# A mixture-of-experts layer beside spiking attention: finding each expert's rows by inverting the permutation on chip and gathering them, in place of scattering them to a sorted table

## The chip, the cores and the metric

The kernel runs on one core of a Trainium2 chip. The metric is the time of one execution on the device, in microseconds (us). Engines are named as in the profile: PE (TensorE), DVE (VectorE), ACT (ScalarE), POOL (GpSimd) and SP (SyncE, which only issues DMAs here). Each engine works through its own program in order and waits on semaphores for the others.

## The reference, cut to what matters

The input is `x` of shape (2, 2048, 256): 4096 tokens. Both halves read the normalized rows `xn` and are added to `x`.

```python
xn = (x - mean(x)) / sqrt(var(x) + 1e-5)
# attention: spikes of layer-normed projections, 16 heads, a distance bias, no softmax
Q, K, V = (lif(layer_norm(xn @ W.T + b, g, beta), 1.0) for each of q, k, v)
out = lif(((16 - hamming(Q, K) + log_pe_bias) * scale) @ V, 0.5)
attn = lif(layer_norm(out @ Wo.T + bo, go, betao), 1.0)
# experts: 8 of them, each token goes to its 2 best
probs = softmax(xn @ router_w.T)
scores, expert_idx = top_k(probs, 2); scores /= sum(scores)
h = xn @ up_proj[e]                      # 256 -> 512
hidden = silu(h[..., :256]) * h[..., 256:]
ffn = sum over the 2 experts of score * (hidden @ down_proj[e])
result = x + attn + ffn
```

Each expert computes only the rows that chose it. There are 8192 (token, choice) pairs. They are sorted by expert and each expert's share is padded to a multiple of 128, so that they fill `SLOT_TILES` = 71 tiles of 128 slots (9088 slots, 896 of them pads).

## The kernel before, in words

A token tile is 128 tokens; there are `NT` = 32, and even and odd tiles belong to the two batches. The program has four stretches.

1. Load and route. `x` is loaded into `xn` and normalized there (`stats`, L768), turned by PE into `xT`, multiplied with the router weights and turned back (L1105 to L1130). DVE picks the two best experts of each token (`pick`), PE counts with a triangular matrix (`ranks`), and DVE works out for each token and choice the slot in the sorted order: `pos`, written at L882, which signals `placed`.
2. Projections. `project_and_sum` on PE, one token tile a step: 3 groups (q, k, v) of a bias matmul (L1160) and six weight matmuls (`three`, L1085 to L1087, a high and a low half of each operand), the turn of the q spikes of the tile four steps back (L1148) and its share of the k-v sum (L1169). ACT keeps the high half of the next tile (`keep_xh`, L432), squares the results (L479) and keeps the turned q (L467). DVE subtracts for the low half (`keep_xl`, L776), finishes the deviations (L924 to L930) and compares for spikes (L941); `project` on DVE handles in step t the spikes of the pair before. `project` on PE for tile t waits for the low half of tile t, and for the spikes of tile t-4, since two sets of three PSUM banks are shared in turn. Between steps ACT and DVE split the expert weights into halves (L436, L918). DVE calls `rest_of_routing` (L886 to L906) between the first pair's spikes and step 4: it finds the owner of each slot tile, and where the pads go.
3. Experts, 71 slot tiles. While the projections run, POOL scatters: for each token tile and each choice an indirect DMA writes 128 rows of `xn` to their slots of the DRAM table `slot_x` (L658, 64 of them), and 7 more write pad rows (L665). Each row carries two more columns: where its result goes, and its first expert. SP waits for all of the scatter (`scattered`) and then loads the table tile by tile into four places `ex` (L340, `load_tile`), each as soon as PE has turned the tile that lay there. PE turns a tile (`turn_ex`, L1212) two tiles ahead, ACT and DVE keep its halves (L524, L910), PE multiplies up, ACT and DVE apply silu and the product (L519, L973), PE turns and multiplies down, ACT stores `ey` (L535), and POOL sends the rows to their places in `slot_y` with an indirect DMA (L673, `send`). DVE computes the destinations of the rows from the two columns (`row_places`, L987). ACT's `keep_y` waits until the send four tiles back has landed. `xres`, the input again for the last addition, is loaded between the tiles (L350).
4. Attention over 16 blocks of 128 positions of both batches, then output projection and the three additions. SP loads `y_tok` from `slot_y` when every send has landed (L366). POOL takes part with L684, L692 and L699.

The order on each engine is written out by hand, with hardware loops (`steps`, `Fori`) where steps repeat. The DVE steps around the change stand so:

```python
deviations(0, 0, 0); spikes(0, 0, 0); keep_xl(4, 4); spikes(0, 0, 1)
dve.wait_ge(s["bias_set"], 1)
rest_of_routing()
for lo, hi, n in PIECE_ROUNDS:      # (4, 16, 8), (16, 28, 14)
    steps(dve, lo, hi, ... project ...)
```

Of the kernel before, what the change touches and what calls it, by code (L numbers as in the profile page):

```python
# [16 lines left out]
P = 128  # L17
# [11 lines left out]
PADS = SLOTS - B * N * TOPK  # L29
PC = PADS // P  # L30
ROW = D + 2
Y_ROWS = TOPK * B * N + 2 * PADS
# [8 lines left out]
BELOW_ALL = -3.0e38  # L41
OFFSETS = [0, 1, -1, 2, -2, 4, -4, 8, -8]
WARM = 16
POOL_PIECES = 8
PEEL, ROUND = 4, 4
KV_OPEN = 2
PIECE_SETS = [(0, 8), (8, 18), (18, 22), (22, PIECES)]
WEIGHT_PIECE, LGT_PIECE, BIAS_PIECE, ROUTE_PIECE, PAD_PIECE = 8, 12, 16, 18, 22
# [3 lines left out]
PAD_TILE = 3  # L52
# [15 lines left out]
def spiking_moe(nc, x, w_all, router, bias, gain, beta, scale, experts, ident, ident_b, toep, far_map, far_pick,  # L68
                head_mask, before, route_const, pad_mark, out):
    with ExitStack() as ctx:  # L70
# [4 lines left out]
        slot_x = nc.dram_tensor("slot_x", (SLOTS, ROW), F32, kind="Internal").ap()  # L75
# [4 lines left out]
        slot_x_tiles = slot_x.rearrange("(j p) d -> p j d", p=P)  # L80
        y_pairs = slot_y[0:TOPK * B * N, :].rearrange("(b a p k) d -> p a b (k d)", b=B, a=NB, k=TOPK)
# [36 lines left out]
        pos = keep("pos", [P, TOPK, NT], I32)  # L118
        owner_f = keep("owner_f", [P, SLOT_TILES])
        owner = keep("owner", [P, SLOT_TILES], I32)  # L120
        pad_i = keep("pad_i", [P, PC], I32)
# [4 lines left out]
        dest = keep("dest", [P, 4], I32)  # L126
# [4 lines left out]
        xn = place_in(r_x)("xn", [P, NT, ROW])  # L131
        xres = place_in(r_x)("xres", [P, NT, D])

# [29 lines left out]
        pos_f = put("pos_f", [P, TOPK, NT])  # L163
# [3 lines left out]
        pad_w = put("pad_w", [P, PC, E])  # L167
        pad_f = put("pad_f", [P, PC])
        rc = put("rc", [P, route_const.shape[1]])
        assert ends[piece_at(ROUTE_PIECE)] <= piece_at(PAD_PIECE)  # L170
        put = place_in(piece_at(PAD_PIECE))
        pad_rows = put("pad_rows", [P, PC, ROW])
        w_rt = put("w_rt", [P, KC, E])
        assert ends[piece_at(PAD_PIECE)] <= piece_at(PIECES)
# [4 lines left out]


# [11 lines left out]
        ex = place_in(r_e)("ex", [P, 4, ROW])  # L192
# [27 lines left out]
        def part(bank, h):  # L220
# [8 lines left out]
        q_ps = banks[6][:, 0:P].bitcast(BF16)  # L229
        kv_ps = banks[7]  # L230
# [13 lines left out]
            chosen_set ranked gap_set gate_exp gates_set placed pads_placed pads_marked pads_done scattered  # L244
            q_turned xh_set xl_set qT_set proj_done ssq_done std_done heron spk_done kv_done
            piece_h piece_l pool_piece far_built far_set half_summed kv_less kv_set kv_fixed
            ex_turned exh_set exl_set sends_begun up_done gact_done hid_done hid_turned hidh_set hidl_set down_done ey_done dest_done
# [6 lines left out]
        ex_in = [sem(f"ex_in{i}") for i in range(4)]  # L254
        y_out = [sem(f"y_out{i}") for i in range(4)]
# [50 lines left out]
        def _(sp):  # L306
# [16 lines left out]
            load_pieces(0)  # L323
            sp.wait_ge(s["routed"], 1)
            sp.wait_ge(s["xn_done"], NT)
# [4 lines left out]
            sp.wait_ge(s["pads_placed"], 1)  # L330
            load_pieces(2)
            sp.wait_ge(s["pads_done"], 16 * PC)
# [3 lines left out]
            def load_tile(j, slot):  # L336
                if not early(j, 4):
                    sp.wait_ge(s["ex_turned"], j - 3)
                    sp.wait_ge(s["dest_done"], j - 3)
                sp.dma_start(ex[:, slot, :], entry(slot_x_tiles, j)).then_inc(ex_in[slot], 16)  # L340

            sp.wait_ge(s["scattered"], 16 * TOPK * NT)
            for j in range(8):
                load_tile(j, j % 4)
# [4 lines left out]
            with sp.Fori(0, QUADS - 2) as i:  # L349
                sp.dma_start(xres[:, bass.ds(i * B, B), :], x_pairs[:, bass.ds(i, 1), :, :].rearrange("p a b d -> p (a b) d")).then_inc(s["xres_in"], 16)  # L350
                for u in range(4):
                    load_tile(i * 4 + (8 + u), u)
            for j in range(4 * QUADS, SLOT_TILES):
                load_tile(j, j % 4)
            for a in range(QUADS - 2, NB):
                sp.dma_start(xres[:, a * B:(a + 1) * B, :], x_pairs[:, a, :, :]).then_inc(s["xres_in"], 16)
# [1070 lines left out]
```

## Time and profile before

| what | us |
|---|---|
| median of 3 runs | 443.77 (443.08 to 443.96) |
| the profiled execution | 444.79 |
| its span, first to last instruction | 442.9 |
| PE busy | 378.5 (85%) |
| DVE, ACT, POOL busy | 273.0, 232.5, 214.5 |

The profiled execution took 444.79 us, of which the profile's span covers 442.9; 1.9 us lie around it. Times in the views are us from the start of the span. PE's matmuls are pipelined, so a busy PE is not PE at its peak. The "granted clock" is the share of full speed that the chip gave PE; 0.5 is 1.2 GHz and 1.0 is 2.4 GHz.

### The profile page before, as it was taken

What the parts mean: (1) busy time and instruction counts of PE and PEld (TensorE: products, weight loads), DVE (VectorE), ACT (ScalarE), POOL (GpSimd) and SP (SyncE); (2) the same over time, 40 slices, a digit from 0 to 9 for tenths busy, and PEclk for the clock granted to TensorE, in tenths of its full rate; (3) what the DMA queues carried; (4) which work ended last, traced back from release to release, by engine and by line L of the source; (5) the groups of instructions that cost most, each with busy time, mean ns of one, the idle gap of its engine ahead of it and who ended that gap; (6) DMA issues with size and microseconds to landing.
All of it is one profiled execution on the core that took longest, in us unless ns stands there. A gap on an engine that the chain in (4) does not pass through costs nothing.

```text
span 442.9 us, 9338 instructions
## 1 busy us (share of the span) xinstructions
PE 378.5 (85%) x2521; PEld 306.0 (69%) x2522; DVE 273.0 (62%) x774; ACT 232.5 (52%) x752; POOL 214.5 (48%) x213
## 2 busy tenths in 40 slices
PE   5388958999999508999999999999999998999840
PEld 1223657999999506778888888888888875666630
DVE  5796899777778505454445545444554434479994
ACT  1436835888888504544455455445445434466650
POOL 5215336777777750333333333333333332489993
PEclk9796979999999956999999999999999999999995
DMA  8880063424222231533334334333334413982222
GB/s 256 257 285 1 10 228 101 174 91 150 95 101 103 95 109 48 169 118 122 119 125 124 119 119 130 120 122 126 121 119 121 115 61 109 382 319 96 95 73 95
DMA packets 40108, 58.93 MB, mean 133 GB/s; under 512 B 5974, under 2 KB 27606, under 8 KB 40088
## 3 DMA queue, kind: packets, MB, share of 16 engines
q1 hardware_dynamic: 31392, 38.53, 27.6%
q0 software_dynamic: 6848, 18.70, 11.6%
q10 hardware_dynamic: 1848, 1.47, 1.1%
q8 instruction: 9, 0.15, 0.1%
q14 instruction: 11, 0.09, 0.1%
HBM read 35.79 MB, written 22.89 MB: 132 GB/s over the span
## 4 chain that ended last, share of the span: by engine, by line
PE 41%; POOL 26%; issue 13%; DMA 6%; DVE 5%; ACT 4%; SPq 3%; DVEq 0%; POOLq 0%; ACTq 0%
POOL slot_x L658 14%; PE bank L1085 12%; PE bank L1087 11%; PE bank L1086 11%; POOL xres L699 4%; POOL xres L692 3%; SPq L309 3%; PE bank L1212 3%; PE bank L1228 3%; DMA ew_f<-experts 2%; DMA vec_d<-two_col 2%; DVE exT_l L910 2%; POOL slot_x L665 2%; ACT gact L519 2%; DMA ex<-slot_x 1%
## 5 line engine op out<-in xcount | busy, mean ns | idle before, releaser
L673 POOL DMA_INDIRECT slot_y<-ey,dest x71 | 68.5, 965 | 139.7 <-ACT ey L535 111.4
L973 DVE TENSOR_TENSOR hid<-gact,bank 128x256 f32<-128x256 f32 x71 | 29.9, 421 | 77.6 <-ACT gact L519 77.6
L658 POOL DMA_INDIRECT slot_x<-xn,pos x64 | 64.7, 1011 | 25.6 <-issue 19.2
L1085 PE MATMUL bank<-ew,exT_h 128*128 x142 | 63.6, 448 | 5.3 <-DVE exT_l L910 5.2
L519 ACT ACTIVATE gact<-bank 128x256 f32<-128x256 f32 x71 | 27.4, 386 | 65.7 <-PE bank L1087 65.7
L1087 PE MATMUL bank<-ew,exT_l 128*128 x142 | 56.9, 401 | 0.0
L1086 PE MATMUL bank<-ew,exT_h 128*128 x142 | 56.8, 400 | 0.0
L1085 PE MATMUL bank<-w_h,xT_h 128*128 128x256 f32 x192 | 54.3, 283 | 0.0
L1087 PE MATMUL bank<-w_h,xT_l 128*128 128x256 f32 x192 | 54.1, 282 | 0.0
L1086 PE MATMUL bank<-w_l,xT_h 128*128 128x256 f32 x192 | 54.1, 282 | 0.0
L1085 PE MATMUL bank<-ew,hidT_h 128*128 x142 | 45.7, 322 | 1.0 <-DVE hidT_l L977 1.0
L479 ACT ACTIVATE junk<-bank 128x256 bf16<-128x256 f32 x96 | 35.8, 379 | 19.3 <-PE bank L1087 18.9
L529 ACT ACTIVATE hidT_h<-bank 128x256 fp32r<-128x256 f32 x71 | 27.3, 385 | 33.5 <-PE bank L1228 33.5
L977 DVE TENSOR_TENSOR hidT_l<-bank,hidT_h 128x256 fp32r<-128x256 f32 x71 | 30.1, 425 | 21.3 <-ACT hidT_h L529 21.3
L1212 PE MATMUL bank<-id_f,ex 128*128 128x128 f32 x142 | 27.7, 279 | 15.9 <-DMA ex<-slot_x 15.9
L910 DVE TENSOR_TENSOR exT_l<-bank,exT_h 128x256 fp32r<-128x256 f32 x71 | 29.7, 418 | 17.4 <-ACT exT_h L524 17.4
L1087 PE MATMUL bank<-ew,hidT_l 128*128 x142 | 40.0, 281 | 0.0
L1086 PE MATMUL bank<-ew,hidT_h 128*128 x142 | 39.9, 281 | 0.0
L1212 PEld LDWEIGHTS bank<-id_f,ex 128*128 128x128 f32 x142 | 20.2, 144 | 26.2 <-DMA ex<-slot_x 16.5
L1085 PEld LDWEIGHTS bank<-w_h,xT_h 128*128 128x128 f32 x192 | 37.3, 194 | 0.0
L1086 PEld LDWEIGHTS bank<-w_l,xT_h 128*128 128x128 f32 x192 | 37.1, 193 | 0.0
L1087 PEld LDWEIGHTS bank<-w_h,xT_l 128*128 128x128 f32 x192 | 37.0, 193 | 0.0
(183 smaller groups left out, 967.4 us busy)
## 6 DMA issues: line engine op xcount, KB each, us to landing
ex<-slot_x SPq DMA_DIRECT2D x71, 129.0 KB, 2.0
y_tok<-slot_y SPq DMA_DIRECT2D x8, 1024.0 KB, 14.1
xres<-x SPq DMA_DIRECT2D x16, 256.0 KB, 2.7
out<-xres SPq DMA_DIRECT2D x16, 256.0 KB, 2.1
xn<-x SPq DMA_DIRECT2D x6, 512.0 KB, 11.7
ew_f<-experts SPq DMA_DIRECT2D x1, 2560.0 KB, 10.1
ew_f<-experts SPq DMA_DIRECT2D x1, 2048.0 KB, 10.3
slot_y<-ey,dest POOLq DMA_INDIRECT x71, 2.4
```

Source lines behind the costliest of these rows:

```text
L479: nc.scalar.activation(junk[:, i, :], proj_ps[r][i], ACT.Square, accum_out=ssq[:, r, i:i + 1]).then_inc(s["ssq_done"], 1)
L519: nc.scalar.activation(gact[:, m % 2, :], h_ps[m % 2][:, 0:F], ACT.Silu).then_inc(s["gact_done"], 1)
L529: nc.scalar.activation(flat2(hidT_h[:, m % 2, :, :]), hT_ps[m % 2], ACT.Copy).then_inc(s["hidh_set"], 1)
L658: pool.indirect_dma_start(slot_x, bass.IndirectOffsetOnAxis(ap=pos[:, k, t:t + 1], axis=0), xn[:, t, :], None).then_inc(s["scattered"], 16)
L673: pool.indirect_dma_start(slot_y, bass.IndirectOffsetOnAxis(ap=dest[:, m % 4:m % 4 + 1], axis=0), ey[:, m % 4, :], None).then_inc(y_out[m ...
L910: v.tensor_tensor(flat2(exT_l[:, m % 2, :, :]), ex_ps[m % 2], flat2(exT_h[:, m % 2, :, :]).bitcast(F32), ALU.subtract).then_inc(s["exl_set ...
L973: v.tensor_tensor(hid[:, m % 2, :], gact[:, m % 2, :], h_ps[m % 2][:, F:2 * F], ALU.mult).then_inc(s["hid_done"], 1)
L977: v.tensor_tensor(flat2(hidT_l[:, m % 2, :, :]), hT_ps[m % 2], flat2(hidT_h[:, m % 2, :, :]).bitcast(F32), ALU.subtract).then_inc(s["hidl_ ...
L1085: mm(dst, a_h, b_h, start=first, stop=False)
L1086: mm(dst, a_h, b_l, start=False, stop=False)
L1087: return mm(dst, a_l, b_h, start=False, stop=last)
L1212: last = turn(ex_ps[m % 2][:, c * P:(c + 1) * P], ex[:, u, c * P:(c + 1) * P], id_f[:, :])
```

## The change

The table `slot_x`, the scatter, the pad rows and the two extra columns go. Instead the normalized rows are written plainly to a DRAM copy `xn_d`, and each slot tile is gathered from it by the slots' token numbers. For that the map from tokens to slots has to be inverted. For each of 64 (choice, token tile) pairs DVE builds two one-hot masks, `in_row` (128 tokens by 128 lanes: the slot's place in its tile) and `in_tile` (128 tokens by 71 tiles, once times the pair's number and once times the token's lane), and PE multiplies the one with the other and sums all 64 products in `inv_ps` (128 lanes by 142). This is done in 4 sets of 16, spread over the DVE steps 4 to 7, which are written out now; PE does its 64 matmuls after step 7 and waits there until DVE has read the result. From it DVE computes `token` (what to gather) and `dest` (where the result goes) for all slots at once. POOL gathers 32 tiles into a ring that lies where `xn` lay, then one more after each send. SP copies a gathered tile from the ring to `ex`. `xres` lies over the ring, and is loaded after the last tile.

```diff
+Y_FIRST = 2 * P
+SETS = 4
+PER_SET = TOPK * NT // SETS
+A_PLACES = 3
+RING = NT
-PEEL, ROUND = 4, 4
+PEEL, TURN_STEP, ROUND = 4, 8, 4
...
         @block.sync
             load_pieces(0)
+            for lo, hi in X_CHUNKS:
+                sp.wait_ge(s["xn_done"], hi)
+                sp.dma_start(xn_rows[:, lo:hi, :], xn[:, lo:hi, :]).then_inc(s["xn_out"], 16)
...
-            sp.wait_ge(s["pads_placed"], 1)
+            sp.wait_ge(s["slots_set"], 2)
+            sp.wait_ge(s["owners_set"], 1)
+            sp.wait_ge(s["turned_back"], SETS)
             load_pieces(2)
...
-                if not early(j, 4):
-                    sp.wait_ge(s["ex_turned"], j - 3)
-                    sp.wait_ge(s["dest_done"], j - 3)
-                sp.dma_start(ex[:, slot, :], entry(slot_x_tiles, j)).then_inc(ex_in[slot], 16)
-            sp.wait_ge(s["scattered"], 16 * TOPK * NT)
+                sp.wait_ge(gathered[j % 4], 16 * (j // 4 + 1))
+                if j >= 4:
+                    sp.wait_ge(s["ex_turned"], j - 3)
+                sp.dma_start(ex[:, j % 4, :], xn[:, j % RING, :]).then_inc(ex_in[j % 4], 16)
...
+            for j in range(8, SLOT_TILES):
+                load_tile(j)
+            blocks = [*range((SLOT_TILES - 2 * RING) // B + 1, NB), *range((SLOT_TILES - 2 * RING) // B + 1)]
+            for a in blocks:
+                last = max(k for k in range(SLOT_TILES) if k % RING in (B * a, B * a + 1))
+                sp.wait_ge(s["ex_turned"], last + 1)
                 sp.dma_start(xres[:, a * B:(a + 1) * B, :], x_pairs[:, a, :, :]).then_inc(s["xres_in"], 16)
...
         @block.scalar
+            def scale_in_tile(c):
+                act.wait_ge(s["in_tile_seen"], c + 1)
+                flat = in_tile[:, c, :, 1, :]
+                nc.scalar.activation(flat, flat, ACT.Copy, scale=p_col).then_inc(s["in_tile_set"], 1)
...
+                    for t in range(lo, TURN_STEP):
+                        project(t, t, n + (t - lo) // 2 if t % 2 else None)
+                        scale_in_tile(t - lo)
...
         @block.gpsimd
-            pool.wait_ge(s["placed"], 1)
-            for t in range(NT):
-                for k in range(TOPK):
-                    pool.indirect_dma_start(slot_x, bass.IndirectOffsetOnAxis(ap=pos[:, k, t:t + 1], axis=0),
-                                            xn[:, t, :], None).then_inc(s["scattered"], 16)
...
+            def gather(j):
+                if j >= 4:
+                    pool.wait_ge(gathered[j % 4], 16 * (j // 4))
+                pool.indirect_dma_start(xn[:, j % RING, :], None, xn_d,
+                                        bass.IndirectOffsetOnAxis(ap=token[:, j:j + 1], axis=0)).then_inc(gathered[j % 4], 16)
...
+            pool.wait_ge(s["slots_set"], 2)
+            for j in range(RING):
+                gather(j)
+            for j in range(SLOT_TILES):
+                send(j)
+                if RING + j < SLOT_TILES:
+                    gather(RING + j)
...
         @block.vector
-            v.tensor_copy(pos[:, :, :], pos_f[:, :, :]).then_inc(s["placed"], 1)
-            def rest_of_routing():
...
+            step(v.tensor_copy(pos_i[:, :], pos_f[:, :]))
+            settled()
+            step(v.tensor_scalar(lo_i[:, :], pos_i[:, :], P - 1, None, ALU.bitwise_and))
+            settled()
+            step(v.tensor_copy(lo_f[:, :], lo_i[:, :]))
+            settled()
+            v.tensor_tensor(hi_f[:, :], pos_f[:, :], lo_f[:, :], ALU.subtract).then_inc(s["split"], 1)
+            def mark_tiles(c):
...
+                shape = [P, PER_SET, SLOT_TILES]
+                step(v.tensor_tensor(in_tile[:, c, :, 1, :], hi_f[:, k].unsqueeze(2).broadcast_to(shape),
+                                     tile_start.unsqueeze(1).broadcast_to(shape), ALU.is_equal))
                 settled()
+                v.tensor_tensor(in_tile[:, c, :, 0, :], in_tile[:, c, :, 1, :], choice_no[:, k].unsqueeze(2).broadcast_to(shape),
+                                ALU.mult).then_inc(s["in_tile_seen"], 1)
+            def mark_rows(c):
+                if c >= A_PLACES:
+                    dve.wait_ge(s["turned_back"], c - A_PLACES + 1)
+                k = slice(c * PER_SET, (c + 1) * PER_SET)
+                shape = [P, PER_SET, P]
+                v.tensor_tensor(in_row[:, c % A_PLACES, :, :], lo_f[:, k].unsqueeze(2).broadcast_to(shape),
+                                row_no.unsqueeze(1).broadcast_to(shape), ALU.is_equal).then_inc(s["in_row_set"], 1)
+            def owners():
...
+            def slots():
+                dve.wait_ge(s["turned_back"], SETS)
...
+                v.tensor_scalar(token[:, :], place, -float(P), 0.0, ALU.add, ALU.max).then_inc(s["slots_set"], 1)
+                v.scalar_tensor_tensor(dest[:, :], place, 2.0, pads, ALU.mult, ALU.add).then_inc(s["slots_set"], 1)
...
-            rest_of_routing()
...
+                    for t in range(lo, TURN_STEP):
+                        mark_tiles(t - lo)
+                        if t - lo < A_PLACES:
+                            mark_rows(t - lo)
+                        project(t, t, None, n + (t - lo) // 2 if t % 2 else None)
+                    owners()
+                    mark_rows(A_PLACES)
+                    slots()
...
-                row_places(j, m, i)
...
         @block.tensor
+            def turn_back(c):
+                if c == 0:
+                    pe.wait_ge(s["qT_set"], TURN_STEP - PEEL)
+                pe.wait_ge(s["in_row_set"], c + 1)
+                pe.wait_ge(s["in_tile_set"], c + 1)
+                for i in range(PER_SET):
+                    last = mm(inv_ps, in_row[:, c % A_PLACES, i, :], in_tile[:, c, i, :, :].rearrange("p a j -> p (a j)"),
+                              start=(c == 0 and i == 0), stop=(c == SETS - 1 and i == PER_SET - 1))
+                last.then_inc(s["turned_back"], 1)
...
-            steps(pe, PEEL, LAST_STEPS, project_and_sum)
+            for t in range(PEEL, TURN_STEP):
+                project_and_sum(t, t, None)
+            for c in range(SETS):
+                turn_back(c)
+            pe.wait_ge(s["slots_read"], 1)
+            steps(pe, TURN_STEP, LAST_STEPS, project_and_sum)
```

`owners` is three of the instructions of `rest_of_routing` (L890, L898, L901). `slots` has three dependent steps of 71 elements ahead of the two that are shown, and the last of the three signals `slots_read`. The masks are bf16, `hi_f`, `lo_f`, `tile_start`, `choice_no` and `row_no` are fp32.

## Rows read from the trace of the kernel before

**Rows 1.** The page, busy time of PE, its share and its instructions.
```profile
PE 378.5 (85%) x2521; PEld 306.0 (69%) x2522; DVE 273.0 (62%) x774; ACT 232.5 (52%) x752; POOL 214.5 (48%) x213
```

**Rows 2.** Chain of work that ended last: start, length, what.
```profile
22.74 10.31 DMA ew_f<-experts
...
68.65 1.06 POOL slot_x L658
...
161.44 2.51 DMA slot_x<-xn,pos
163.97 2.10 DMA ex<-slot_x
166.12 0.70 PE bank L1212 x2
```

**Rows 3.** PE timeline: start, length, line, tiles, count, idle before and its releaser.
```profile
75.27 0.38 PE L1160 MATMUL bank<-bias_r,ones_r 128*128 128x256 f32 x1 [1.34 <-DVE xT_l L776]
...
83.38 0.36 PE L1160 MATMUL bank<-bias_r,ones_r 128*128 128x256 f32 x1
...
149.07 0.28 PE L1169 MATMUL bank<-v_spk,qk_spk 128*128 128x128 bf16 x2
149.19 0.28 PE L1148 MATMUL bank<-id_b,qk_spk 128*128 128x128 bf16 x2
...
150.96 0.27 PE L1169 MATMUL bank<-v_spk,qk_spk 128*128 128x128 bf16 x2
...
175.43 0.48 PE L1085 MATMUL bank<-ew,exT_h 128*128 x1
...
186.00 0.48 PE L1085 MATMUL bank<-ew,exT_h 128*128 x1
...
190.10 0.48 PE L1085 MATMUL bank<-ew,exT_h 128*128 x1
```

**Rows 4.** Windows: stretch, busy time of the engines, granted clock, DMA share, GB/s.
```profile
57.50:61.30 3.80, 0.00 (x0) 0.01 (x1) 3.61 (x7) 2.46 (x8) 1.75 (x2) 0.97 1.03 384
61.30:68.00 6.70, 5.85 (x27) 5.39 (x28) 6.39 (x19) 1.22 (x5) 1.00 (x1) 0.51 0.16 62
...
151.20:166.10 14.90, 0.03 (x1) 0.00 (x0) 0.00 (x0) 0.34 (x1) 8.64 (x9) 0.57 0.32 108
...
167.90:173.60 5.70, 5.66 (x14) 4.34 (x15) 4.06 (x12) 1.82 (x3) 0.00 (x0) 0.50 0.05 9
...
200.00:280.00 80.00, 78.07 (x480) 67.11 (x478) 39.23 (x120) 39.56 (x120) 28.80 (x30) 1.00 0.39 122
```

**Rows 5.** DVE timeline from the routing to step 5 of the projections.
```profile
68.17 0.20 DVE L882 CAST pos<-pos_f 128x64 int32<-128x64 f32 x1
...
71.67 0.16 DVE L886 TENSOR_TENSOR per_e<-per_e 128x8 f32<-128x8 f32 x1
...
71.95 0.67 DVE L890 TENSOR_TENSOR owner_w<-rc,per_e 128x497 f32<-128x497 f32 x1
...
74.71 0.42 DVE L776 TENSOR_TENSOR xT_l<-xT,xT_h 128x256 fp32r<-128x256 f32 x1 [0.26 <-issue]
...
78.59 0.69 DVE L918 TENSOR_TENSOR ew<-ew_f,ew  x1
```

**Rows 6.** Groups by line: tiles, shapes, count, busy, mean ns, idle before.
```profile
L673 POOL DMA_INDIRECT slot_y<-ey,dest x71 | 68.5, 965 | 139.7 <-ACT ey L535 111.4 <-issue 28.3
L658 POOL DMA_INDIRECT slot_x<-xn,pos x64 | 64.7, 1011 | 25.6 <-issue 19.2 <-DVE pos L882 6.4
...
L436 ACT ACTIVATE ew<-ew_f 128x512 fp32r<-128x512 f32 (+1 forms) x24 | 14.7, 620 | 5.0 <-DMA ew_f<-experts 5.0
```

**Rows 7.** DVE timeline where the experts begin.
```profile
167.25 0.42 DVE L910 TENSOR_TENSOR exT_l<-bank,exT_h 128x256 fp32r<-128x256 f32 x1 [17.11 <-ACT exT_h L524]
...
169.47 0.42 DVE L910 TENSOR_TENSOR exT_l<-bank,exT_h 128x256 fp32r<-128x256 f32 x1
```

**Rows 8.** SP's queue, timeline: first issue, time to the last, tiles, count.
```profile
372.19 13.88 SPq L366 DMA_DIRECT2D y_tok<-slot_y  x8
```

More of the change, by code:

```diff
@@ L68, in spiking_moe @@
 def spiking_moe(nc, x, w_all, router, bias, gain, beta, scale, experts, ident, ident_b, toep, far_map, far_pick,
-                head_mask, before, route_const, pad_mark, out):
+                head_mask, before, route_const, out):
     with ExitStack() as ctx:
@@ L117, in spiking_moe @@
         gwork = keep("gwork", [P, 3, NT])
[L118 to L119 removed]
         owner = keep("owner", [P, SLOT_TILES], I32)
[L121 removed]
+        token = keep("token", [P, SLOT_TILES], I32)
+        dest = keep("dest", [P, SLOT_TILES], I32)
         eps_c = keep("eps_c", [P, 1])
@@ L162, in spiking_moe @@
         best = put("best", [P, 4, NT])
-        pos_f = put("pos_f", [P, TOPK, NT])
+        pos_f = put("pos_f", [P, TOPK * NT])
+        lo_f, hi_f = (put(n, [P, TOPK * NT]) for n in ("lo_f", "hi_f"))
+        pos_i = put("pos_i", [P, TOPK * NT], I32)
+        lo_i, hi_i = (put(n, [P, TOPK * NT], I32) for n in ("lo_i", "hi_i"))
+        slot_w = put("slot_w", [P, 4, SLOT_TILES])
         per_e = put("per_e", [P, 8, E])
@@ L178, in spiking_moe @@
         spk = put("spk", [P, NB, B, D])
+        at = sum(CONST_WIDTHS[:4])
+        choice_no = rc[:, at:at + TOPK * NT]
+        row_no = rc[:, at + TOPK * NT:at + TOPK * NT + P]
+        p_col = rc[:, at + TOPK * NT + P:at + TOPK * NT + P + 1]
         r_v = ends[r_w]
@@ L254, in spiking_moe @@
         ex_in = [sem(f"ex_in{i}") for i in range(4)]
+        gathered = [sem(f"gathered{i}") for i in range(4)]
         y_out = [sem(f"y_out{i}") for i in range(4)]
@@ L348, in _ @@
             sp.dma_start(far_s[:, :], far_map).then_inc(s["toep_in"], 16)
[L349 to L355, printed above, removed]
+            for j in range(8, SLOT_TILES):
+                load_tile(j)
+            blocks = [*range((SLOT_TILES - 2 * RING) // B + 1, NB), *range((SLOT_TILES - 2 * RING) // B + 1)]
+            for a in blocks:
+                last = max(k for k in range(SLOT_TILES) if k % RING in (B * a, B * a + 1))
+                sp.wait_ge(s["ex_turned"], last + 1)
                 sp.dma_start(xres[:, a * B:(a + 1) * B, :], x_pairs[:, a, :, :]).then_inc(s["xres_in"], 16)
@@ L620, in _ @@
             g.memset(ones_b[:, :], 1.0).then_inc(s["ones_set"], 1)
-            step(g.memset(pad_rows[:, :, :], 0.0))
             step(g.memset(ones_r[:, :].bitcast(F32), 1.0))
@@ L810, in _ @@
             consts = []
-            for width in (E, E * NT, SLOT_TILES, PC, NT):
+            for width in CONST_WIDTHS[:4]:
                 consts.append(rc[:, at:at + width])
                 at += width
-            rev, keep_run, tile_start, pad_no, y_place = consts
-            step(v.tensor_copy(xn[:, :, D], y_place))
+            rev, keep_run, tile_start, pad_row = consts
             all_te = [P, NT, E]
@@ L839, in _ @@
             step(v.scalar_tensor_tensor(lg2[:, :, :], first[:, :, :], BELOW_ALL, lg, ALU.mult, ALU.add))
-            step(v.tensor_scalar(xn[:, :, D + 1], best[:, 1, :], -1.0, float(E), ALU.mult, ALU.add))
             settled()
@@ L978, in keep_hidl @@
                                 ALU.subtract).then_inc(s["hidl_set"], 1)
-            def row_places(j, m, i):
-                u = m % 4
-                if early(j, 4):
-                    dve.wait_ge(ex_in[u], 16)
-                else:
-                    dve.wait_ge(y_out[u], 16 * i)
-                v.scalar_tensor_tensor(dest[:, u:u + 1], ex[:, u, D + 1:D + 2], cut(owner_f, j, 1), ex[:, u, D:D + 1],
-                                       ALU.not_equal, ALU.add).then_inc(s["dest_done"], 1)
             def expert(j, m, i):
```

112 lines of the change are left out of this document (53 added, 59 removed).

## The prediction

> **What bounds the kernel now.** I read the page first: PE is busy for 85% of the span [rows 1], so a PE idle stretch is what a change can win, and added PE waits are what it can lose. The chain of waits names the idle stretch: from 68.65 it runs through POOL's scatter, 64 + 7 indirect DMAs back to back, to the last one at 161.44; that lands after 2.51, the first tile load takes 2.10, and only then, at 166.12, does PE turn the first expert tile [rows 2]. The PE timeline gives the other side: the last projection work ends at 151.1 [rows 3], so PE stands still for 15.0 us; the window 151.2 to 166.1 has no PE work in it [rows 4]. The next window shows the after-effect: when PE restarts, the granted clock is 0.50 (the 1.2 GHz level) for 5.7 us [rows 4]. From 200 to 280 PE is busy for 78.07 of 80 us at full clock, 480 matmuls, 16 a tile: 30 tiles at 2.67 us each [rows 4]. The experts are bound by PE. Projections are too: from step 8 (83.38) to the end of step 31 (149.07) are 24 steps of 2.74 us [rows 3]. There the DVE timeline matters: two DVE steps (4 and 5) start at 74.71 and end at about 79.2, so 4.5 for two, 2.25 each [rows 5]. DVE has 0.5 us to spare per step of PE. That small reserve is what the new masks draw on.
>
> **What is won where the experts begin.** With the scatter gone, PE passes from the last projection to the first turn at 151.1 instead of 166.12. I follow the same order of instructions at full clock, in times of the old trace. The first low half starts on DVE about 0.9 after that turn begins (1.13 in the trace with the turn at half clock), at 152.0. The second follows 2.2 later, since the last spikes lie between them (167.25 to 169.47, at DVE's own speed [rows 7]), and PE can start its second tile at 154.8. The two tiles' up matmuls took 5.7 at half clock [rows 4], so one takes 1.4 at full; the turn of the last q spikes, an exchange with ACT, took the 1.8 from 173.6 to the third tile at 175.43 [rows 3, 4]. The third tile then starts at 154.8 + 1.4 + 1.8 = 158.0 instead of 175.43: **17.4 won**, 15.0 of waiting and 2.4 of clock. Bounds: 15.0 if PE comes out of the handover at half clock again, 18.5 if its small waits shrink too.
>
> A second gain: the step from tile 6 at 186.00 to tile 7 at 190.10 took 4.10 instead of 2.67 [rows 3], because the tile load stood in SP's queue behind two tables and a part of `xres`. That part moves to the end, and the load no longer waits for `row_places`. **1.4 won**, bounds 0 and 1.4. The removed `row_places` itself is worth nothing: DVE is busy for 39 of 80 us there [rows 4].
>
> **What the masks cost.** They stand in DVE's program between steps that feed PE. The price per element: a compare of 497 elements took 0.67 and an instruction of 8 took 0.16 [rows 5], so 0.16 fixed and 1.04 ns an element. `mark_tiles` is two instructions of 16 x 71 = 1136 elements, 1.35 each, the second waiting for the first: 2.7. `mark_rows` is one of 2048, 2.3, or 2.2 to the next start. Four sets: 4 x (2.7 + 2.2) = 19.5. No mask is in the old trace; below, two results a cycle would give 10; above, 25, if POOL or a broadcast operand slowed them. I take 19.5, by the nearest row, a compare with broadcast operands.
>
> DVE's program now, from the same start: `rest_of_routing` began at 71.67 [rows 5]. Splitting the slot number adds three small dependent instructions like L882's 0.20 [rows 5] and two small copies go: 72.1. Then 19.5 of masks, 9.0 for four steps, and 1.6 for `owners` (two instructions like L890's 0.67 and a small one [rows 5]): 102.2. The last set's 16 matmuls follow on PE: two bf16 matmuls of 128 columns start 0.12 apart [rows 3], so 142 columns take 0.067, the set 1.1. Then DVE's chain up to `slots_read`, four small instructions or waits of 0.2: 0.8. PE begins step 8 at 104.1 instead of 83.38: **20.7 lost**. PE steps 5 to 7 each wait for a low half behind the masks, as step 5 does already for 1.34 [rows 3]. The first three sets (3.3, or 6.6 at half clock) lie under DVE's step 7 and `owners`; with all of it at half clock PE ends later than DVE and the loss is 22.5. Bounds 19 and 22.5 before any clock loss behind it. Nothing is given back later, because steps 8 to 31 run at PE's pace.
>
> The waits have this queue behind them: behind PE's wait for `slots_read` stand all later projections; behind `mark_rows(3)`, waiting for the first set, stand `slots` and DVE's step 8. ACT's four scalings of 1136 elements, 1.4 each if 512 take 0.62 [rows 6], fall where ACT waits for PE; uncovered they would cost 5.5.
>
> The clock: after 3.8 us without PE work (57.5 to 61.3) it was granted 0.51 for 6.7 us, about 3.3 us of work lost [rows 4]. In the new steps 5 to 7 PE stands for 4 to 5 us between projections, so it will fall there, where DVE sets the pace. Behind step 8 it costs 0 if it has recovered during the sets, 3.3 if not. I take **1.0**.
>
> **Parts that I cost at nothing.** The gathers begin at 104.5; 32 at 1.01 + 0.30 [rows 6] end at 146.5, 25 us before the experts. Without that cover each would cost its 1.3. In the expert stretch POOL does a send and a gather a tile for 39 tiles: 0.97 + 0.30 + 1.31 = 2.58 against PE's 2.67 [rows 4, 6]. A gather is not in the trace: below, it is a send's 0.97, above the 2.51 from issue to landing [rows 2]; I take the scatter's, the same instruction the other way round. The plain copy of `xn` (4 MB) is issued behind the load of expert pieces at 22.74, which takes 10.31 [rows 2]; if it stays behind in the same queue it costs nothing and is out by about 50, if it mixed in, up to 4 us. `xres`, again 4 MB, is issued once tile 66 is turned, some 26 us ahead of the reading of `y_tok` at 372.19 [rows 8]; at the 384 GB/s of one window [rows 4] it takes 11. Uncovered: 11. The Trainium skill, in "DMA: Bandwidth & Descriptors", section Queues, rings and completion order, says that each DMA engine takes turns between the queues of the issuers. By it the last sends would share the engines with `xres` and not wait behind all of it, which leaves the sum as it is; no run so far shows it.
>
> **Sum**, for the profiled execution: 444.8 + 20.7 + 1.0 - 17.4 - 1.4 = 447.7. The old median lies 1.0 below its profiled execution, so I forecast **446.7** for the median, 2.9 above the old. By 0.2% (0.9 us), what a measurement of this kernel can tell from no change, that is slower.
>
> **Rivals.** (B) The masks cost less, and the kernel gets faster. Place: DVE in steps 4 to 7. Everything else being as above, it decides from a mask sum below 16.6 instead of 19.5. For it: the masks are written in bf16. Against it: their inputs are fp32, and the compare of 497 elements ran at one a cycle. At two a cycle the masks take 10.2, and the median is 446.7 - 9.3 = 437.4. The Trainium skill, in "VectorE: DVE Perf Modes", section The perf-mode tier table, gives an operation on two tensors twice the rate for bf16 and the single rate for fp32. By the first the time would be the 437.4, by the second my sum; L890 with fp32 on both sides agrees with the second, and bf16 results from fp32 inputs no quiet row shows. (C) PE comes back at half clock at step 8, or in the handover, and pays another 3: 449.5. For it: both earlier restarts did so [rows 4]. Against it: the sets themselves are PE work just ahead. (D) POOL cannot keep the pace: from 1.40 a gather the pair is longer than 2.67. At 1.7 it falls behind by 0.3 a tile, 11.7 in 39 tiles; `keep_y` tolerates a send some three tiles late, 7 us: about 5 more, 451.7. Against it: the scatter's even 1.31. (E) The copy of `xn` delays the expert pieces, on which the early chain hangs [rows 2], by up to 4: 450.7. (F) The change doesn't free the start of the experts, because a gathered tile comes late: the 17.4 stay away and it is 464. The 25 us of cover speak against it.
>
> **How the numbers follow.** The forecast (A) has 0.63, with its own range 443.5 to 449.5; B 0.12, C 0.12, D 0.07, E 0.04, F 0.02. Of A, 0.13 lies at faster (masks or routing shorter by a fifth) and 0.08 within 0.2%; B is faster, and half a share of C to E is eaten by a shorter mask sum, 0.02. Faster 0.27, same 0.09, slower 0.64. The range goes from 440.0, half of B left out, to 452.0, which takes in C, E and most of D.
>
> **What would show it.** Right: PE's step 8 at 104 to 106; the compares at 1.35 and 2.3; PE waiting for DVE three times by 4 to 5 us between 77 and 102; no idle stretch at the experts' start, and full clock there; gathers at 1.3, over by 147; 2.67 a tile as before; the last stretch unchanged. Wrong: masks at 0.7 and 1.2; PE idle ahead of the expert tiles; a tile pace above 2.7 in the first 39 tiles; `ew_f` landing later than 33.

## The result and the profile after

The changed kernel takes **449.37 us** (median of 4, 448.21 to 450.83), the kernel before 443.42 beside it (4 runs, 441.89 to 443.96): a ratio of 1.0153, 95% interval 1.0134 to 1.0173. It is slower by 5.95 us, where I forecast 2.9: right in sign and inside the range, too small by half.

From the page of the changed kernel, the same line as in [rows 1]. TensorE is busy 11 us longer, in 64 more matmuls and in work at the lower clock:
```profile
PE 389.5 (87%) x2585; PEld 318.6 (71%) x2586; DVE 283.8 (64%) x717; ACT 237.0 (53%) x756; POOL 210.7 (47%) x211
```
DVE's timeline, the first set of masks, the next set's first mask, and the last mask with what follows. It answers to [rows 5]; columns are start, length, engine, line, operation, tiles, shapes, and in brackets the idle time before and its releaser:
```profile
72.27 1.34 DVE L916 TENSOR_TENSOR in_tile<-hi_f,rc 128x1136 bf16<-128x1136 f32 x1
73.64 1.35 DVE L919 TENSOR_TENSOR in_tile<-in_tile,rc 128x1136 bf16<-128x1136 bf16 x1
74.90 2.29 DVE L928 TENSOR_TENSOR in_row<-lo_f,rc 128x2048 bf16<-128x2048 f32 x1
...
79.31 1.34 DVE L916 TENSOR_TENSOR in_tile<-hi_f,rc 128x1136 bf16<-128x1136 f32 x1
...
99.55 2.28 DVE L928 TENSOR_TENSOR in_row<-lo_f,rc 128x2048 bf16<-128x2048 f32 x1
104.00 0.23 DVE L945 TENSOR_SCALAR slot_w<-bank 128x71 f32<-128x71 f32 x1 [2.17 <-PE bank L1246]
```
PE's timeline over the same stretch and to tile 7 of the experts, for [rows 3]: the starts of steps 5, 6 and 7, the sets of matmuls that invert the permutation, step 8 and step 9, the last group of step 31, the third expert tile, and the tiles 6 and 7 (counted from 0, as in the prediction):
```profile
77.58 0.38 PE L1207 MATMUL bank<-bias_r,ones_r 128*128 128x256 f32 x1 [2.89 <-DVE xT_l L796]
...
85.09 0.55 PE L1207 MATMUL bank<-bias_r,ones_r 128*128 128x256 f32 x1 [3.01 <-DVE v_spk L990]
...
91.56 0.49 PE L1207 MATMUL bank<-bias_r,ones_r 128*128 128x256 f32 x1 [2.07 <-DVE xT_l L796]
...
95.78 3.21 PE L1246 MATMUL bank<-in_tile,in_row 128*128 128x142 bf16 x48
101.89 2.07 PE L1246 MATMUL bank<-in_tile,in_row 128*128 128x142 bf16 x16 [2.90 <-DVE in_row L928]
105.27 0.39 PE L1195 MATMUL bank<-id_b,qk_spk 128*128 128x128 bf16 x2 [1.30 <-DVE slot_w L950]
...
105.48 0.58 PE L1207 MATMUL bank<-bias_r,ones_r 128*128 128x256 f32 x1
...
109.72 0.36 PE L1207 MATMUL bank<-bias_r,ones_r 128*128 128x256 f32 x1
...
173.21 0.28 PE L1207 MATMUL bank<-bias_r,ones_r 128*128 128x256 f32 x1
...
183.01 0.48 PE L1132 MATMUL bank<-ew,exT_h 128*128 x1
...
193.52 0.48 PE L1132 MATMUL bank<-ew,exT_h 128*128 x1
...
196.05 0.49 PE L1132 MATMUL bank<-ew,exT_h 128*128 x1
```
Windows of the changed kernel, for [rows 4] (stretch, busy time of PE, PEld, DVE, ACT, POOL, then the granted clock, DMA share and GB/s):
```profile
95.00:102.00 7.00, 4.10 (x59) 3.87 (x58) 6.77 (x10) 2.28 (x6) 0.00 (x0) 0.99 0.00 0
102.00:105.00 3.00, 1.97 (x16) 1.68 (x15) 0.93 (x5) 0.00 (x0) 0.00 (x0) 0.50 0.00 0
105.00:112.00 7.00, 6.73 (x46) 6.61 (x47) 3.59 (x14) 3.46 (x13) 4.02 (x4) 0.73 0.76 261
112.00:173.00 61.00, 61.00 (x546) 59.79 (x546) 47.53 (x143) 50.05 (x198) 27.57 (x28) 1.00 0.25 74
173.00:185.00 12.00, 8.74 (x62) 7.05 (x61) 8.27 (x23) 6.68 (x22) 0.00 (x0) 1.00 0.18 56
200.00:280.00 80.00, 78.32 (x483) 67.48 (x482) 35.34 (x90) 39.56 (x120) 58.53 (x61) 1.00 0.45 146
```
POOL at the start of the gathers and in the expert stretch, for [rows 6]:
```profile
105.79 1.17 POOL L682 DMA_INDIRECT xn<-xn_d,token  x1 [43.65 <-DVE dest L955]
107.26 0.95 POOL L682 DMA_INDIRECT xn<-xn_d,token  x1 [0.30 <-issue]
...
187.31 1.00 POOL L688 DMA_INDIRECT slot_y<-ey,dest  x1 [38.67 <-ACT ey L562]
188.62 0.98 POOL L682 DMA_INDIRECT xn<-xn_d,token  x1 [0.30 <-issue]
189.90 1.00 POOL L688 DMA_INDIRECT slot_y<-ey,dest  x1 [0.30 <-issue]
```
The difference, stretch by stretch on PE, after against before:

| stretch | before | after | difference |
|---|---|---|---|
| start to step 8 | 83.38 | 105.48 | +22.1 |
| step 8 to the last group of step 31 | 64.89 | 67.73 | +2.8 |
| last group to the third expert tile | 27.16 | 9.80 | -17.4 |
| third tile to tile 6 | 10.57 | 10.51 | -0.1 |
| tile 6 to tile 7 | 4.10 | 2.53 | -1.6 |
| tile 7 to the last matmul of the experts | 177.01 | 176.17 | -0.8 |
| from there to POOL's last addition into `xres` | 69.73 | 70.23 | +0.5 |

(In the trace of before the last group of step 31 starts at 148.27, the last matmul of the experts at 367.11 and that addition ends at 436.84; after, 372.22 and 442.45.) The sum is +5.6, close to the medians' 5.95. The two profiled spans differ by 3.4 only, since from that last addition to the end the trace of before takes 6.1 and this one 3.9. The traces of all the variants below take 3.8 to 3.9 there; whether 6.1 is usual for the kernel before, its one trace doesn't tell. Its profiled execution (444.79) lies 1.4 above its median, that of the changed kernel (448.21) 1.2 below.

### The profile page after: what moved, and what is told of

It is laid out like the page before. It is cut to its first block, busy times and chain, and to the rows that moved or that the text cites. A ratio compares the mean times of both kernels' runs of the same rounds, so it can differ in the third digit from the quotient of the medians.

```text
span 446.3 us, 8933 instructions
## 1 busy us (share of the span) xinstructions
PE 389.5 (87%) x2585; PEld 318.6 (71%) x2586; DVE 283.8 (64%) x717; ACT 237.0 (53%) x756; POOL 210.7 (47%) x211
## 4 chain that ended last, share of the span: by engine, by line
PE 55%; DVE 15%; issue 9%; POOL 9%; DMA 4%; ACT 3%; SPq 3%; POOLq 0%; DVEq 0%; ACTq 0%
PE bank L1132 15%; PE bank L1134 14%; PE bank L1133 14%; POOL xres L719 4%; POOL xres L712 3%; PE bank L1291 3%; SPq L323 3%; DMA ew_f<-experts 2%; PE bank L1275 2%; PE bank L1207 2%; DVE in_row L928 2%; DMA vec_d<-two_col 2%; DVE exT_l L959 2%; ACT gact L546 2%; POOL rstd L704 1%
## 5 line engine op out<-in xcount | busy, mean ns | idle before, releaser
L682 POOL DMA_INDIRECT xn<-xn_d,token x71 | 69.5, 978 | 66.8 <-DVE dest L955 43.6
L1031 DVE TENSOR_TENSOR hid<-gact,bank 128x256 f32<-128x256 f32 x71 | 29.9, 421 | 77.2 <-ACT gact L546 77.2
L1132 PE MATMUL bank<-w_h,xT_h 128*128 128x256 f32 x192 | 57.4, 299 | 0.0
L1133 PE MATMUL bank<-w_l,xT_h 128*128 128x256 f32 x192 | 57.2, 298 | 0.0
L1134 PE MATMUL bank<-w_h,xT_l 128*128 128x256 f32 x192 | 57.1, 297 | 0.0
L1132 PEld LDWEIGHTS bank<-w_h,xT_h 128*128 128x128 f32 x192 | 40.0, 208 | 0.0
L1207 PE MATMUL bank<-bias_r,ones_r 128*128 128x256 f32 x96 | 31.4, 327 | 9.6 <-DVE xT_l L796 5.8
L1133 PEld LDWEIGHTS bank<-w_l,xT_h 128*128 128x128 f32 x192 | 39.7, 207 | 0.0
L1134 PEld LDWEIGHTS bank<-w_h,xT_l 128*128 128x128 f32 x192 | 39.5, 206 | 0.0
L1132 PEld LDWEIGHTS bank<-ew,exT_h 128*128 128x128 f32 x142 | 26.7, 188 | 12.8 <-issue 9.6
L1134 PEld LDWEIGHTS bank<-ew,exT_l 128*128 128x128 f32 x142 | 26.7, 188 | 6.0
```

The costliest lines, as they stand in the source:

```text
L682: pool.indirect_dma_start(xn[:, j % RING, :], None, xn_d, bass.IndirectOffsetOnAxis(ap=token[:, j:j + 1], axis=0)).then_inc(gathered[j % 4 ...
L1031: v.tensor_tensor(hid[:, m % 2, :], gact[:, m % 2, :], h_ps[m % 2][:, F:2 * F], ALU.mult).then_inc(s["hid_done"], 1)
L1132: mm(dst, a_h, b_h, start=first, stop=False)
L1133: mm(dst, a_h, b_l, start=False, stop=False)
L1134: return mm(dst, a_l, b_h, start=False, stop=last)
L1207: mm(proj_ps[r][i], ones_r[:, :], bias_r[:, cols], start=True, stop=False)
```

## The experiments

Steps 4 to 8, then the pace behind them, were longer than forecast. My theory by then: the inversion costs what VectorE's instructions take; its end adds a half clock that I had put at 1.0; and the projections became slower by an address effect that no part of the change intends. "Medians differ by" means against 449.4; beside it stands the same from the ratios to the kernel before, which takes out what chips differ by. "Either way" is half of a 95% interval.

**The masks, doubled.**
```
+v.tensor_tensor(in_row[...], lo_f.., row_no.., ALU.is_equal)      # once more, in each set
 v.tensor_tensor(in_row[...], lo_f.., row_no.., ALU.is_equal)
```


> The changed kernel with the lane compare in_row (128x2048, 2.29 us) issued twice in each of the four sets. Theory A (VectorE's instructions alone set the time of steps 4 to 7): each of the four sets comes 2.3 us later and the time rises by 4 x 2.3 = 9.2 us, to 458.5. Theory B (part of the loss is waits on other engines, ScalarE's scaling or TensorE's matmuls, under which a longer VectorE would hide): the time rises by less than 7 us, below 456.5.


Measured: 458.14 us, ratio 1.0336 (1.0308 to 1.0364). Medians differ by +8.8, ratios by +8.1 (1.5 either way), of 9.2 added. DVE's timeline of this kernel shows the pair and the set behind it:
```profile
75.23 2.28 DVE L928 TENSOR_TENSOR in_row<-lo_f,rc 128x2048 bf16<-128x2048 f32 x1
77.55 2.29 DVE L931 TENSOR_TENSOR in_row<-lo_f,rc 128x2048 bf16<-128x2048 f32 x1
81.97 1.33 DVE L916 TENSOR_TENSOR in_tile<-hi_f,rc 128x1136 bf16<-128x1136 f32 x1
```
The next set starts at 81.97 where it started at 79.31; 0.3 of the difference was there before the pair (75.23 against 74.90), 2.3 is the second compare. In the whole trace step 8 starts at 115.05 in place of 105.48, 9.6 later. Theory A holds: steps 4 to 7 go at VectorE's pace and nothing hides a mask. It is the trace that decides, since by the ratios alone theory B's 7 would still be possible.

**No inversion.**
```
-    mark_tiles(..); mark_rows(..)           # VectorE       -    scale_in_tile(..)      # ScalarE
-    turn_back(c), wait for slots_read       # TensorE
+    token = slot number & 4095; dest = Y_FIRST + slot number     # from the constants
```


> Leaves the inversion out: no masks on VectorE, no scaling on ScalarE, no 64 matmuls; the gathers' row numbers come from a constant table after the owners (slot number within the 4096 tokens), so the rows are not each expert's own, while count and size of gathers and sends are those of the changed kernel. Theory A (the inversion costs what the trace shows between steps 4 and 9: 22.1 us up to step 8 and 1.4 us of half clock behind it): 449.4 - 23.5 = 425.9, which is 17.5 below the kernel before, the gain at the experts' start and at tile 6 to 7 alone. Theory B (a rival: hidden behind the masks lies a second cost, the gathers or code loading, that ends as late): the time falls by less than 20 us, above 429.4.


Measured: 425.71, ratio 0.9603 (0.9577 to 0.9629): medians 23.7 below, ratios 24.4 (1.5 either way). The forecast of 425.9 was met, and no second cost stands behind the masks. The gathers are still there, but begin at 86.1 in place of 105.8, so a cost of theirs wouldn't show in this run; the table above has no stretch that they lengthen. This is also the price list of the change: the early start of the experts gains 17, the inversion as placed takes back 24.

**The masks with 16-bit inputs** (rival B of the prediction, by itself).
```
-    lo_f, hi_f, tile_start, row_no, choice_no in f32
+    lo_h, hi_h, start_h, row_h, choice_h in bf16
```


> The changed kernel with every input of the masks' instructions in bf16 (positions, lane numbers, tile starts and choice numbers are whole numbers that bf16 holds), which costs three more casts; the broadcasts of an operand over its last or middle dimension stay. Rival B of the prediction (16-bit operands double VectorE's rate): in_tile compare and product 0.75 each in place of 1.34, the lane compare 1.2 in place of 2.29, 2.3 us less in each of four sets: 449.4 - 9.2 + 0.4 = 440.6. The other theory (an operand broadcast over its last dimension keeps VectorE at one element a cycle, whatever its type): the three instructions stay at 1.34, 1.34 and 2.29 and the time at 449.4 to 449.9.


DVE's timeline of this kernel:
```profile
73.27 1.33 DVE L922 TENSOR_TENSOR in_tile<-hi_h,start_h 128x1136 bf16<-128x1136 bf16 x1
74.63 1.35 DVE L925 TENSOR_TENSOR in_tile<-in_tile,choice_h 128x1136 bf16<-128x1136 bf16 x1
75.89 2.28 DVE L934 TENSOR_TENSOR in_row<-lo_h,row_h 128x2048 bf16<-128x2048 bf16 x1
```
All three take what they took with fp32 inputs, to 0.01 us (1.34, 1.35 and 2.29). The time (515.05, ratio 0.9965, 0.9939 to 0.9990) comes from another chip, on which the kernel before took 515.93, and says little; the instructions' lengths decide. Rival B falls in its stronger form too: bf16 everywhere does not bring these masks to the double rate. In the two compares both inputs are broadcast, one over its last dimension and one over its middle one. In the product (L925) only `choice_h` is, over its last dimension, and it takes 1.35 all the same, so one such input goes with the single rate. A mask without a broadcast was not run.

**TensorE kept busy at the end of the inversion.**
```
     turn_back(2)
+    44 matmuls 128x128 bf16 that nothing reads
     turn_back(3)
+    wait until the spikes have left the bank that is written next
+    20 more
     wait for slots_read
```


> The changed kernel with matmuls that nothing reads, to fill TensorE's stops at the end of the inversion: 44 of 128x128 bf16 after the third set (where it stood 2.90 us) and 20 after the fourth (where it stood 1.3 us and more). Nothing that VectorE waits for changes, save that the fourth set may start later. Theory A (the granted clock went to 0.50 because TensorE stood still there, and that is the half clock behind which the fourth set took 2.07 us in place of some 1.05 and step 8 took 4.24 us in place of 2.8): the fourth set falls to about 1.1 us, step 8 to 2.8 and the time by 2.0 to 2.4 us, 449.4 to about 447.2. Rival (the clock is granted by something else, or the filling matmuls come at half clock themselves and delay the fourth set): no gain, 449.4 to 450.5.


Measured: 446.87, ratio 1.0078 (1.0054 to 1.0103): medians 2.5 below, ratios 3.3 (1.4 either way). PE's timeline of this kernel, then two windows of it:
```profile
99.24 2.62 PE L1258 MATMUL bank<-id_b 128*128 128x128 bf16 x44
102.27 1.19 PE L1246 MATMUL bank<-in_tile,in_row 128*128 128x142 bf16 x16 [0.41 <-DVE in_row L928]
103.30 1.28 PE L1258 MATMUL bank<-id_b 128*128 128x128 bf16 x20
...
104.97 0.38 PE L1207 MATMUL bank<-bias_r,ones_r 128*128 128x256 f32 x1
...
107.79 0.36 PE L1207 MATMUL bank<-bias_r,ones_r 128*128 128x256 f32 x1
```
```profile
102.00:105.00 3.00, 2.55 (x39) 2.29 (x39) 1.52 (x8) 0.00 (x0) 0.00 (x0) 1.00 0.00 0
105.00:112.00 7.00, 7.00 (x63) 6.91 (x63) 4.39 (x13) 4.71 (x19) 4.10 (x4) 1.00 0.83 286
```
The clock is granted in full (2.4 GHz) where it was at 0.50, the fourth set takes 1.19 for 2.07, step 8 takes 2.82 (104.97 to 107.79) for 4.24. Work that nobody needs made the kernel faster: the half clock came from TensorE's stops at the end of the inversion, and by these rows it cost 0.9 + 1.4 = 2.3. (Step 9 starts 1.9 earlier, at 107.79 in place of 109.72, since the last mask ended 0.4 later in this execution.) The two fillings were tried together only.

**The addresses.** In the changed kernel the groups of a projection come 0.83 us apart, before 0.79. The kernel without the inversion has 0.83 too, and in the changed kernel it goes on after the last gather (148.6), so neither masks nor gathers do it. The change had made tiles smaller in SBUF (the on-chip memory that the engines read from) and so moved all that lies behind them.
```
     junk = keep("junk", ...)
+    keep("hole_a", 64 B)
     xn = place_in(r_x)("xn", ...)
+    place_in(r_x)("hole_b", [P, NT, D + 2])      # the size of the old slot region
     ex = place_in(r_e)("ex", [P, 4, D])
+    place_in(r_e)("hole_c", [P, 4, D + 2])       # 64 B more than ex
```


> The changed kernel with three unused holes in SBUF (64 B, one of the size that the region of xn lost, and 64 B in the region of the experts), so that the projections' operands (w_h, w_l, xT_h and the others) lie at the addresses that they had before the change; no instruction differs. In the changed kernel the groups of a projection from step 9 on come 0.83 us apart where they came 0.79 to 0.80 apart before, some 1.4 us over steps 9 to 28. Theory A (the addresses, shifted by 320 and 384 B, cost the pace): the groups come 0.79 to 0.80 apart again, the mean projection matmul goes from 299 back to about 283 ns, and the time falls by 1.4 to 1.6 us, from 449.4 to about 447.9. Theory B (something else, as where the code lies or the longer program): pace and time stay, 449.4 within 0.4.


Measured: 447.19, ratio 1.0095 (1.0077 to 1.0113): medians 2.2 below, ratios 2.6 (1.2 either way). Theory A holds: the groups are back at 0.79. In its trace steps 9 to 31, from the first to the last group, take 62.1 us in place of 63.5 (before 62.1), the whole of the projections 119.5 in place of 121.1. The 1.4 to 1.6 of this lie within what the ratios allow; that it is more, as the medians would have it, is not shown. Which part of the address counts, four runs with fewer holes tell:


> Of the three holes only the two of 64 B (in the region of constants and in the experts' region): w_h, w_l and xT_h now lie 256 B, and 256 B alone, below their addresses of before. Theory A (what counts is the position within 128 or 256 B, which the two odd 64 B changed): the groups of a projection come 0.79 us apart as with all three holes. Theory B (the 256 B matter too, or alone): they stay at 0.83.

> Of the three holes only the large one, which gives back the 256 B: w_h and w_l lie 64 B and xT_h 128 B below their addresses of before. Theory A (the position within 128 or 256 B counts): 0.83 stays as in the changed kernel. Theory B (the 256 B matter): 0.79.

> Which operand's address counts. One hole of 64 B, in the constants' region: w_h and w_l lie at a multiple of 128 B, as before the change, and xT_h and xT_l at a multiple of 128 B too (before: 64 B above one; in the changed kernel all four lie 64 B above one). Theory A (the moving operands w_h, w_l must lie at a multiple of 128 B): groups 0.79 us apart. Theory B (the weights xT_h, xT_l must lie 64 B above one): 0.83.

> The other half: one hole of 64 B, in the experts' region, so that w_h and w_l lie 64 B above a multiple of 128 B as in the changed kernel, and xT_h and xT_l at a multiple. Theory A (the moving operands count): groups 0.83 us apart. Theory B (weights and moving operands must lie on different sides of the 128 B): 0.79.


(b3 and b4 ran on the chip of the bf16 masks and took 513.39 and 512.29, each once; the bf16 masks, with the addresses of the change, have 0.83 there too.) Two neighbouring groups in each trace, the starts to be subtracted: the changed kernel, all holes, then b3, b4, d1 and d2:
```profile
127.50 0.28 PE L1207 MATMUL bank<-bias_r,ones_r 128*128 128x256 f32 x1
128.33 0.28 PE L1207 MATMUL bank<-bias_r,ones_r 128*128 128x256 f32 x1
```
```profile
126.23 0.28 PE L1210 MATMUL bank<-bias_r,ones_r 128*128 128x256 f32 x1
127.02 0.28 PE L1210 MATMUL bank<-bias_r,ones_r 128*128 128x256 f32 x1
```
```profile
166.60 0.28 PE L1209 MATMUL bank<-bias_r,ones_r 128*128 128x256 f32 x1
167.39 0.28 PE L1209 MATMUL bank<-bias_r,ones_r 128*128 128x256 f32 x1
```
```profile
165.08 0.28 PE L1208 MATMUL bank<-bias_r,ones_r 128*128 128x256 f32 x1
165.91 0.28 PE L1208 MATMUL bank<-bias_r,ones_r 128*128 128x256 f32 x1
```
```profile
125.44 0.28 PE L1208 MATMUL bank<-bias_r,ones_r 128*128 128x256 f32 x1
126.28 0.28 PE L1208 MATMUL bank<-bias_r,ones_r 128*128 128x256 f32 x1
```
```profile
126.18 0.28 PE L1208 MATMUL bank<-bias_r,ones_r 128*128 128x256 f32 x1
127.00 0.28 PE L1208 MATMUL bank<-bias_r,ones_r 128*128 128x256 f32 x1
```

| kernel | w_h, w_l (moving): bytes above a multiple of 128 | xT_h, xT_l (weights) | group |
|---|---|---|---|
| before; all holes; b3 (256 B lower) | 0 | 64 | 0.79 to 0.80 |
| changed; b4 (256 B given back) | 64 | 64 | 0.83 |
| d1 | 0 | 0 | 0.83 to 0.84 |
| d2 | 64 | 0 | 0.82 |

(Counted from the start of the kernel's part of SBUF.) A shift by 256 B changes nothing, one by 64 B does. My theory for d1, that the moving operand alone decides, fell: with `w` back at a multiple of 128 the pace stayed at 0.83 to 0.84. Of d2 the theory that the two need only lie on different sides fell as well. Of the four combinations only the one of before is fast. Each hole moves everything behind it, though, and not these operands alone; that it is they is argued, since the seven matmuls of a group read nothing else that moved. Why it is so, the traces don't show; nor why the first steps, at 52 to 57 us, had 0.82 before, 0.84 changed and 0.79 with all holes at the same addresses as before. (d1 took 449.89 and d2 449.13, each once.)

**The inversion spread over steps 4 to 20.**
```
-    all of mark_tiles, mark_rows in steps 4 to 7; the sets in one block ahead of step 8
+    step 4: compare  5: product  6: lane compare, scaling  7: 16 matmuls  8: partial sum kept in SBUF
+    the same from steps 8, 12 and 16 on; owners in 19, slots in 20; 20 gathers ahead of the first send, not 32
```


> The changed kernel with the inversion spread over steps 4 to 20: one mask instruction, one scaling or one set of 16 matmuls a step, each set of matmuls a sum of its own that VectorE adds up in SBUF, the slots at the end of step 20; 20 gathers ahead of the sends in place of 12, since they start some 30 us later. Theory A (VectorE has about 0.5 us free in each of the 16 steps, 8 to 9 us of the masks' 19.5, and TensorE has neither a stop of 2 to 3 us nor a half clock): the loss against before falls from 23.5 to about 11.5 to 15, and the time is 438 to 441, below the 443.4 of the kernel before. Theory B (the spread mask stops every step because VectorE has no room, its total counts): the whole 19.5 stays, about 445 to 446. Theory C (the gathers, now late, end after the first experts' tile wants them): the handover grows from 9.8 us and the time is above 446.


(The "12" in it is wrong: the changed kernel issues 32 gathers ahead of the first send.) Measured: **436.01**, ratio 0.9845 (0.9821 to 0.9870). One set in PE's timeline of this kernel, then the stretch as a window:
```profile
111.83 1.18 PE L1270 MATMUL bank<-in_tile,in_row 128*128 128x142 bf16 x16 [0.87 <-DVE in_row L938]
```
```profile
83.00:139.00 56.00, 50.44 (x466) 48.28 (x465) 54.21 (x132) 39.49 (x151) 4.22 (x4) 1.00 0.09 31
```
DVE is busy for 54.2 of 56 us: its reserve is used up, so it still bounds these steps. But from the first to the last group the projections take 108.1 us, before 96.0, changed 121.1: the inversion costs 12.1 where it cost 25.1, the slower pace of the groups in both. In this window PE never stops for over 0.9 us and the clock stays at 1.00. Theory A holds, 2 us below its range. The gathers end in time, at 161.0, and PE turns the first expert tile at 163.4.

With the holes on top:


> The spread inversion (436.0 us) with the three unused holes of the addresses' run, so that the projections' operands lie where they did before the change. Theory A (the two are independent: the addresses gave 0.0058 of the time of before, 2.6 us, of which the groups' pace over the projections explains some 2): 433.5 to 434.5. Theory B (in the spread kernel steps 4 to 20 are set by VectorE, so a faster TensorE gives only what it gives in the other 12 steps, some 0.9 us): 435.0 to 435.4.


That run fell on the other chip: 490.7 against 515.93 for the kernel before, ratio 0.9492. Repeated:


> The spread inversion with the addresses of before once more, since its first run fell on a chip on which the kernel before took 515.9 us. Theory A (both gains add up): 0.0058 below the spread one's ratio of 0.9845, 0.979 of before, 433.5 on a chip where before takes 442.8. Theory B (steps 4 to 20 are set by VectorE, so a faster TensorE gives 0.9 us): a ratio of 0.9825, 435.1.


Measured: **434.78**, ratio 0.9797 (0.9771 to 0.9823), 8.8 below the kernel before. Against the spread kernel the ratio falls by 0.0048 (0.0036 either way), between A's 0.0058 and B's 0.0020, and neither can be told from it. The traces speak for B: from step 4 to step 21 it takes 58.2 us against 58.6 in the spread kernel, from there to the last group 29.2 against 29.9, so 1.0 in all, and most of it where VectorE doesn't set the pace. The other difference of the two traces lies where the experts begin. Windows of the spread kernel, then of this one:
```profile
163.00:168.00 5.00, 3.90 (x17) 3.01 (x17) 3.65 (x12) 2.43 (x6) 0.00 (x0) 0.69 0.15 52
163.00:168.00 5.00, 3.76 (x21) 2.81 (x20) 3.95 (x14) 2.94 (x6) 0.00 (x0) 1.00 0.21 71
```
The order of work is the same, but PE got the half clock for a part of this stretch in one (clock 0.69) and not in the other: from the last group to the third expert tile 10.8 us against 9.8. Of the 13 traces of kernels with gathers, 7 have 10.7 to 10.9 there and 6 have 9.8, among them the changed kernel's. With one trace of each it stays open whether that differs by kernel or by execution.

## Why the prediction was half right

- **The gain where the experts begin** (17.4) was measured at 17.4, at full clock, and the tile 6 to 7 gain (1.4) at 1.6. Rival F is out. The full clock was in part luck: in 7 of the 13 traces the same stretch takes 1.0 longer at a lower clock.
- **The masks** (four sets of 2.7 and 2.2, 19.5) were right to 0.01 us an instruction, and VectorE was at the end of its last mask at 101.8, as worked out (102.2). Doubling one mask and removing all show that this was the right bound. The sentence on the Trainium skill's "VectorE: DVE Perf Modes", The perf-mode tier table, is borne out for fp32 inputs (1.34 for 1136 elements, 2.29 for 2048). The double rate that its row gives for bf16 did not come with bf16 on both sides (1.33 and 2.28). That is no contradiction: the same page of the Trainium skill, in What auto-detection actually checks, asks for a step of 1 or -1 in every tensor besides 16 bits, and an input broadcast over its last dimension has a step of 0. The prediction used the row without this condition.
- **The failed step is the clock, "I take 1.0".** Against more, the text had the reason that "the sets themselves are PE work just ahead". Three of the four sets were: they ran from 95.78 to 98.99. But then PE stood 2.90 for the last lane compare, and the fourth set and step 8 ran at the half clock (1.2 GHz). That is 1.0 in the set, which the sum had at full clock, and 1.4 in step 8: 2.4 in place of 1.0. Keeping TensorE busy gave 2.3 by its rows and 2.5 to 3.3 by the times. Step 8 began at 105.5 instead of 104.1: the set took 1.0 longer, the chain from there to step 8 took 0.7 longer, and the set began 0.3 earlier. I had seen the two ends (0 and 3.3) and had the rival (C, 449.5), and gave it 0.12. The wait of 2.90 could have been read from my own sum: sets 0 to 2 done by 99, the last mask at 102. (C's figure is not well added up: another 3 on 446.7 is 449.7, and 3.3 in place of the 1.0 gives 449.0.)
- **A term was missing: the projections' pace.** Nothing in the prediction moved addresses. It cost 1.4 us in steps 9 to 31, by the traces with and without the holes. C's 449.5 lies so near to the measured time because this term, of which C has nothing, came on top of a half clock that cost less than C took.
- The sign "PE waiting for DVE three times by 4 to 5 us" did not come: the waits ahead of steps 5 to 7 were 2.9, 3.0 and 2.1. DVE's pace was as forecast; PE worked on these steps at the half clock, as the text also said, and so waited less.
- The costs put at nothing were nothing: a gather took 0.95 + 0.30 (0.97 to 1.01 + 0.30 taken), send and gather 2.58 a tile, as computed, against PE's 2.67; the copy of `xn` and `xres` hid. D and E are out. The small changes at the end, -0.8 over the experts and +0.5 behind them, nearly cancel.

446.7 with the clock at 2.4 instead of 1.0 and 1.4 for the addresses is 449.5, against 449.37 measured. That it fits so well is in part chance: left out of it are 0.4 more ahead of step 8, 0.6 less from the third tile to the end, and the clock at the experts' start, which makes 0 or 1.0.

## What to carry to other kernels

In this kernel a serial block on a helper engine cost its whole length where it stood between steps that feed the bound engine. Spread to at most one mask instruction a step, it cost about half, since the helper's reserve took up the rest and the bound engine kept its clock (25.1 became 12.1). When you sum such a block, also write down where the bound engine stands still just before it restarts, and price that restart at the half clock. After an edit to the memory plan, compare the distance of neighbouring matmul groups in an untouched stretch: it shows whether the pace changed where no instruction did.

## What was not expected of the hardware

- Shifts of 64 B in SBUF: 0.79 against 0.82 to 0.84 us for a group of 7 fp32 matmuls of 256 columns.
- bf16 inputs and output, one or both inputs broadcast: 2.28 us for 2048 elements, 1.35 for 1136, no faster than with fp32 inputs.
- The same short stop ahead of the experts left PE at full clock in 6 traces and at a lower one in 7.
- Chips differ. On one, the kernel before took 515.93 where others gave 442.8 and 443.6. The trace of the bf16 masks from there shows PE waiting for its own instructions while the gathers run, with no engine or DMA named:
```profile
135.55 0.40 PE L1201 MATMUL bank<-id_b,qk_spk 128*128 128x128 bf16 x2 [10.14 <-issue]
```
What takes this time there stays open; each ratio in this text is taken on one chip.
